# A routed-expert layer and the attention behind it: half of the attention's preparation moved ahead of the last gather

## The reference

```python
t = t + _L2_ffn_ref(_ln_t(t), ...)      # 8 experts, top 2 of each token, gelu
t = t + _L3_attn_ref(_ln_t(t), ...)     # one head, 64 wide, over all 1024 tokens
t = t + _L3_ffn_ref(_ln_t(t), ...)      # 8 experts, top 1, capacity 160

def _L3_attn_ref(inputs, W_q, W_k, W_v, W_o, b_o):
    Q = jnp.einsum('bsd,du->bsu', inputs, W_q)
    K = jnp.einsum('bsd,du->bsu', inputs, W_k)
    V = jnp.einsum('bsd,du->bsu', inputs, W_v)
    attn = jnp.einsum('bqu,bku->bqk', Q, K) * scale
    w = jax.nn.softmax(attn, axis=-1)
    out = jnp.einsum('bqk,bku->bqu', w, V)
    return jnp.einsum('bsu,ud->bsd', out, W_o) + b_o + inputs
```

## Time and profile before

| | us |
|---|---|
| median of 3 runs | 527.66 |
| lowest and highest run | 524.83, 527.77 |
| the profiled execution's own time | 527.12 |
| its span in the trace | 525.4 |
| PE busy in the span | 460.5 (88%) |
| DVE busy | 320.3 (61%) |
| ACT busy | 226.0 (43%) |
| POOL busy | 167.7 (32%) |
| mean granted clock of PE | 0.91 |

### The profile page before, as it was taken

One profiled execution on the slowest core, in us unless ns is written; L12 is line 12 of the kernel. 1 busy time (PEld: TensorE's weight loads), 2 busy tenths in 40 slices (PEclk: granted clock), 3 DMA queues, 4 the chain that ended last, 5 costly groups with the idle time before them and its releaser, 6 DMA issues.

```text
span 525.4 us, 10346 instructions
## 1 busy us (share of the span) xinstructions
PE 460.5 (88%) x3619; PEld 346.4 (66%) x3619; DVE 320.3 (61%) x891; ACT 226.0 (43%) x522; POOL 167.7 (32%) x229
## 2 busy tenths in 40 slices
PE   4988999796999999998797887999970999889984
PEld 3276777433577777776677777999960644477973
DVE  3968878477956676947637634672434550557466
ACT  0848787264155655553413204755520234210630
POOL 7722217103412332325213037257716400021000
PEclk9999999899699999999767758999995899969997
DMA  7000000000000000008000033868613100000001
GB/s 289 15 2 2 1 2 1 1 2 1 1 1 1 2 1 1 2 2 320 1 1 1 20 95 87 191 164 197 197 44 121 75 0 0 1 1 0 1 1 40
DMA packets 13692, 24.80 MB, mean 47 GB/s; under 512 B 1954, under 2 KB 7914, under 8 KB 13130
## 3 DMA queue, kind: packets, MB, share of 16 engines
q1 hardware_dynamic: 12170, 21.12, 12.1%
q0 software_dynamic: 1472, 3.02, 3.2%
HBM read 21.12 MB, written 3.01 MB: 46 GB/s over the span
## 4 chain that ended last, share of the span: by engine, by line
PE 74%; DVE 12%; ACT 5%; issue 4%; DMA 1%; POOL 1%; DVEq 1%; POOLq 0%; ACTq 0%
PE ps L1106 67%; PE ps L1249 3%; PE ps L1116 2%; DVE tabs L1830 1%; ACT arena L1030 1%; POOL arena L787 1%; PE ps L1229 1%; DVE st L1813 1%; DMA xT<-in_xT_dram 1%; DVE arena L1958 1%; DVE tabs L1998 1%; PE ps L1565 1%; DVE oK L1934 1%; DVE nmx L2060 1%; DVE st L1794 1%
## 5 line engine op out<-in xcount | busy, mean ns | idle before, releaser
L2060 DVE TENSOR_REDUCE nmx<-ps 128x1 f32<-128x512 f32 x64 | 43.7, 686 | 22.3 <-PE ps L1106 21.9
L949 ACT ACTIVATE pT<-ps 128x512 f32<-128x512 f32 x64 | 38.2, 597 | 40.1 <-PE ps L1106 39.5
L1106 PE MATMUL ps<-kr,qr 128*128 128x320 f32 (+3 forms) x136 | 46.2, 403 | 4.4 <-DVE kr L1985 2.4
L778 POOL DMA_INDIRECT arena<-expert_rows_dram,row_of x30 | 31.1, 1037 | 47.4 <-DVE row_of L2213 37.5
L1030 ACT ACTIVATE arena<-ps,tabs 128x128 f32<-128x128 f32 x120 | 34.1, 369 | 27.4 <-PE ps L1106 25.6
L1958 DVE CUSTOM_DVE_ANT_0 arena<-ps,tabs 128x320 f32<-128x320 f32 (+1 forms) x64 | 28.8, 458 | 14.7 <-PE ps L1106 14.7
L579 POOL TENSOR_TENSOR rstd<-ve,nhalf 128x4 f32<-128x4 f32 (+2 forms) x17 | 15.5, 912 | 62.4 <-DVE ve L1823 62.0
L1106 PE MATMUL ps<-pT,tabs 128*32 128x128 f32 (+2 forms) x576 | 34.7, 293 | 0.7 <-ACT pT L949 0.7
L675 POOL TENSOR_TENSOR tabs<-vaug,ones 128x151 f32<-128x151 f32 x32 | 14.2, 445 | 64.5 <-PE ps L1106 36.7
L1106 PEld LDWEIGHTS ps<-kr,qr 128*128 128x128 f32 x136 | 25.5, 198 | 12.9 <-issue 5.7
L1106 PE MATMUL ps<-fw,arena 128*128 x240 | 32.0, 276 | 1.3 <-ACT arena L1030 1.3
(11 more groups left out here) (356 smaller groups left out, 1124.9 us busy)
## 6 DMA issues: line engine op xcount, KB each, us to landing
fw<-in_m_w_dram SPq DMA_DIRECT2D x3, 2048.0 KB, 8.0
xT<-in_m_w_dram SPq DMA_DIRECT2D x16, 256.0 KB
cT<-in_m_w_dram SPq DMA_DIRECT2D x14, 256.0 KB
expert_out_dram<-arena SPq DMA_DIRECT2D x30, 64.0 KB, 3.3
convw<-in_convw_dram SPq DMA_DIRECT2D x1, 1600.0 KB, 11.1
rows<-in_rows_dram SPq DMA_DIRECT2D x1, 584.0 KB, 7.0
xT<-in_xT_dram SPq DMA_DIRECT2D x1, 512.0 KB, 3.6
expert_rows_dram<-tabs SPq DMA_DIRECT2D x2, 256.0 KB, 4.6
```

The costliest lines, as they stand in the source:

```text
L778: pool.indirect_dma_start(out=x_rows[:, i, :], out_offset=None, in_=x_dram[h], in_offset=bass.IndirectOffsetOnAxis(ap=row_of[:, h, i:i + 1 ...
L949: act.activation(pT[:, u % 8, :], ps[:, 4 + u % 2, :], ACT.Exp).then_inc(S("n1_p"), 1)
L1106: return pe.matmul(dst, lhsT, rhs, start=start, stop=stop, skip_group_check=True)
L2060: dve.tensor_reduce(nmx[:, s // NH8, s % NH8:s % NH8 + 1], ps[:, s % N1_S, :], AX.X, ALU.max, negate=True).then_inc(S("n1_nmx"), 1)
```

## The change

The first half's root stands ahead of `rows_back(1)` on POOL, and its two adds right behind it, ahead of the second half's root. On DVE the first half's normalising and its query and key parts come ahead of combine(2). ACT's copy and parts are done half by half. On PE the first half's transposes, queries, keys and values come right behind the expert loop, then four fillers, a wait for six combined tiles and eight fillers, then the second half. The seven fillers, the wait for eight combined tiles and the four fillers between the transposes are gone. Fillers now write bank 1.

```diff
             pool.wait_ge(*at("n3_ones", 1))
-            rows_back(1)
-            token_roots("nc")
-            for t in range(0, T, 4):
+            def add_last(t):
+
                 v = aK[:, t:t + 4, :]
                 pool.wait_ge(*at("nc_norm", t + 4))
                 link(pool.tensor_tensor(v, v, row("L3_attn_b_o").unsqueeze(1).broadcast_to([P, 4, P]), ALU.add))
                 pool.tensor_tensor(v, v, bK[:, t:t + 4, :], ALU.add).then_inc(S("xb3_ready"), 1)
+
+            token_root("nc", 0)
+            rows_back(1)
+            add_last(0)
+            token_root("nc", 1)
+            add_last(4)
             for i in range(2):
                 pool.wait_ge(*at("n3_k", i + 1))
...
             for i in range(2):
                 turned_half(nT, 0, "nc_tps", "nc_T", i)
-            for i in range(2):
                 act.wait_ge(*at("n3_q_ps", i + 1))
...
             pe.wait_ge(*at("w3_in", 16))
-            warm(7, 3)
-            pe.wait_ge(*at("m2_acc", T))
-            channels_half("nc", 0)
-            warm(4, 3)
-            channels_half("nc", 1)
-            pe.wait_ge(*at("w3_twice", 1))
             for i in range(2):
-
+                channels_half("nc", i)
+                if i == 0:
+                    pe.wait_ge(*at("w3_twice", 1))
                 pe.wait_ge(*at("nc_T", i + 1))
                 for a, name in enumerate(("n3_q_ps", "n3_k_ps")):
                     mm(ps[:, 2 + 2 * a + i, :], w3qk[:, a, :, :].rearrange("p r u -> p (r u)"), halves(nT)[i]).then_inc(S(name), 1)
-            for i in range(2):
                 values_half("n3", i, w3q[:, 2, :], U)
+                if i == 0:
+                    warm(4, 1)
+                    pe.wait_ge(*at("m2_acc", 6))
+                    warm(8, 1)
...
-            combine(2)
-            combine(3)
-
-
             normalise_half("nc", aK, bK, 0)
-            normalise_half("nc", aK, bK, 1)
             for i in range(2):
+                if i:
+                    combine(2)
+                    combine(3)
+                    normalise_half("nc", aK, bK, 1)
                 dve.wait_ge(*at("n3_q_high", i + 1))
...
```

## The result

The changed kernel takes **536.04 us** (median of 4 executions, 532.55 to 538.73) where the kernel before takes 527.39 beside it: a ratio of **1.0171, 95% interval 1.0125 to 1.0218**. It is slower, by some 9 us, where 526.2 was forecast. A second set on another chip gave 536.52 (6 executions, 534.88 to 537.84), ratio 1.0194 (1.0161 to 1.0228). On the chips used later, executions of the kernel before come in two groups, 523 to 529 us (38 of 79) and 533 to 540 (41 of 79); the ratios here leave out what lies over 1.5% above a kernel's own fastest execution, and all ten executions of the changed kernel lie at 532.55 or above.

A forecast was written before the change was run, and what follows sets the result against it. The prediction took the last expert rows' gather to bound the kernel until about 411 us, then PE. Moved work was hidden; the first score came 0.9 us earlier, off 527.12 us: 526.2, range 523.2 to 528.6 (8 in 10).

The forecast's parts named there:

- what was hidden: Around POOL's gathers: the first half's root (1.03 us), its DVE parts and PE's added work fit into waits, costing nothing.
- rival 4: First half's query and key parts on DVE block POOL's gather issues: everything behind 1.38 us later, 527.6 us, chance 0.07.
- the forecast's two: End of PE's fillers ahead of the second half: about 402.8 us at full clock, 407.5 at half.
- the lock: POOL's moved additions lengthen the first operation of combine(3) on DVE by 0.75 us, bounds 0 to 1.0.
- the second normalising: On DVE, four tiles of the second half, freed from POOL's additions: 1.11 us instead of 3.24.
- the gain at the first score: Last attention's first score at 415.44 instead of 416.36 us: 0.9 us gained at half clock.
- moves the rest of the kernel with it: From about 411 us PE sets the end, so an earlier first score brings everything after it forward.
- When the clock rises again is unknown: 4.5 us after the restart, as before: PE in the second half: full clock possibly back at 412.9 us, saving another 0.4 us.
- rival 3: Half clock lasts into the scores, 10.2 us from the restart: scores lose 1.6 us, kernel 527.8 us, chance 0.17.
- No case reaches that on either side: Whole kernel: no case changes the time by about 1%, 5.3 us; same 0.91, faster 0.05, slower 0.04.
- The 10.2-us row: Profile window 462.0 to 472.2 us: PE's clock stayed at 0.50 although PE was busy for 10.10 us.

The follow-up runs named there:

- e7: Changed kernel with more fillers during the gather and in the second half's gaps, POOL's additions behind the second normalising: 529.34 us, ratio 0.9977.
- e4: Changed kernel with eight more fillers between the second half's values and the first score: 529.15 us, ratio 1.0024.
- e14: The same program as e4 again, changed kernel with eight late fillers, twelve executions: 530.08 us, ratio 1.0074.
- e17: Changed kernel with eight float32 fillers contracting over 64 partitions ahead of the first score: 528.95 us, ratio 1.0049.
- e13: Changed kernel again without edit, more executions beside the kernel before on another chip: 536.52 us, ratio 1.0194.
- e8: Changed kernel with six fillers between the second and third tile's scores: 532.12 us in one execution.
- e2: Kernel before without its seven and four fillers in this stage: 531.38 us, ratio 1.0042.
- e9: Changed kernel with both halves' queries, keys and values together behind the second transposes, more gather fillers, POOL's additions behind the second normalising: 526.29 us, ratio 0.9996.
- e3: Changed kernel without its four and eight fillers and without the wait for six combined tiles: 536.96 us, ratio 1.0177.
- e10: e7 with eight instead of three fillers right ahead of the first score: 529.93 us over ten executions, ratio 0.9955.
- e11: Kernel before with eight fillers between its last values product and first score: 527.97, 530.53, 539.22 and 540.90 us, no ratio.
- e12: e9 with four fillers right ahead of the first score: 531.82 us over ten executions, ratio 1.0051.
- e16: Changed kernel with eight fillers of type fp32r ahead of the first score: 531.89 us, ratio 1.0012.

## Why the prediction was wrong, step by step

**Right: what was hidden.** The root ran at 384.27, and POOL then waited 2.87 us for the expert rows. The eight issues kept their step: 9.30 us from first to last after, 9.17 before, although the first half's parts lay beside them, so rival 4's 1.38 us didn't come. The issues took 1.00 to 1.11 us. The Trainium skill's rule on the shared port, page "SBUF — State Buffer", section "SBUF: two separate sides", is about DVE operations in a two-port mode. The parts beside the issues read PSUM, and no run here shows that they are of that kind, so these rows neither bear the rule out nor refute it. The fillers ended at 399.99; shifted by the 2.96 us this is 402.95, the early end of the forecast's two (402.8).

**Right: the lock and the second normalising.** 1.13 us against 0.35, so 0.78 for the forecast's 0.75, and 1.11 for the normalising. e7 shows the cause: without the additions there the operation takes 0.35.

**Right: the gain at the first score.** Forecast 0.9 at half clock; measured 0.80, or, counted from the last issue (397.47 against 400.30, 2.83 earlier), 0.93. What was then taken for granted, that an earlier first score "moves the rest of the kernel with it", did not hold: the end came 6.3 us later.

**Wrong: when the clock comes back.** The step that failed is "When the clock rises again is unknown: 4.5 us after the restart, as before", with the price of rival 3 that stood beside it, 10.2 us from the restart, 1.6 us of loss, chance 0.17. Rival 3's mechanism is what happened. Its price was mis-sized: the clock came back at 440.2, 440.2 - 405.43 = 34.8 us after the restart, and the loss behind the first score is 119.1 - 109.0 = 10.1 us, not 1.6. In the same way "No case reaches that on either side" fell: I bounded what could be lost by the stretch up to the first score, while the stage behind it, whose products had only been seen at full clock, stood open at half price.

Both bounds came from places with other products. The 4.5 us were four transposes and four fillers right ahead of both halves' four query and key products. The change took away just that: it left one half's two (x4) and its four small values products (x8) behind pauses of 5.43 and 0.69 us. The 10.2-us row had already said that a busy PE need not get its clock back; I took its length for a limit, which it was not.

**What is shown and what stays open.** Shown: the scores run at either level with PE busy throughout; losing full clock there costs 8 to 10 us; the changed work by itself does not slow them (e4 against e14, the same program); with eight fillers between the second half's values and the scores the clock was at full at the first score in all five profiles of the changed kernel (e4, e14 to e17), without them at half in both (after, e13); behind six fillers among the scores it was full again after 6.8 us (e8, one execution), where without them the loss lasted 20 us or more; and with both halves' products together, as before, only a part of the executions are as slow (two of four in e2, four of ten in e9), with one half's and no fillers added all of them (after, e13, e3). Not shown: what in PE's work raises the clock, for in e4 and e17 it rose before the fillers and in e9 before the products; what brings it back 27.6 us behind the first score of after; and why scores that begin at full clock hold it in one execution and lose it within 6 us in the next. More fillers ahead of them did not settle it (e10, e11, e12), nor did fillers of the scores' type or size (e16, e17). That the kernel before's own executions at 533 to 540 us are the same fall is likely, but none of them was traced in the score stage. The likeliest reading is that the change makes sure of a loss that before meets only at times: all ten executions against 41 of the 79 above.

## What to carry to other kernels

When work is moved off the path into a wait, ask what it was doing for TensorE's clock where it stood: here taking one half's products away from in front of the scores gained under a microsecond of work and lost some 9 us to the clock. Price the clock not to the end of the stage that changes but to the end of whatever runs next without a break, and take the price from rows with the same products, or leave the range open. A busy PE in a window was no sign here that its clock would rise.

## What the runs showed of the hardware

PE was busy for all of 27.60 us at a granted clock of 0.50, with score products of 0.73 us that take 0.43 at 1.00; e3 shows 27.40 us of the same. And a clock at full was lost in the scores although PE had been busy for 18.76 us before them and stayed so (e10).

The Trainium skill, page "TensorE: Matmul & The Clock Gate", section "What's actually happening", says that PE gets its full clock once it has been busy for a short while. By that, the loss would have ended soon after the first score, as rival 3 had it. The trace disagrees, with these 27.60 us. The same section says that the gate's window runs free of the program, so that one kernel can meet the change at different points. That would fit e4 and e14, whose clock differed with the same instructions; no run here shows that it is the reason.
